# The end of the context attentions of a four-layer gated model: slot 0's head sums, inverses and output product placed between slot 1's column scores

## The chip, the cores and the metric

One core of one Trainium2 chip runs the whole program as one kernel. The metric is the device time of one execution in microseconds (us). TensorE is called PE below, VectorE DVE, ScalarE ACT.

## The reference, cut to what matters

Four gated blocks change `x` of 4 batches x 512 tokens x 128 features. Each block is a cross-attention on a context of 77 rows of 64 features, then a second function (a quantised MLP in the first block, others later). Blocks 0, 1 and 3 attend with 16 heads; block 1's context attention (`a2`) is the second half of a larger function and has 32 features a head, blocks 0 and 3 have 8.

```python
    x = x + jnp.tanh(g_xattn[0]) * _L0_xattn_ref(_layernorm(x, axis=-1), ctx_512, ctx_512, ...)
    x = x + jnp.tanh(g_ffn[0]) * _L0_ffn_ref(_layernorm(x, axis=-1), ...)
...
        scores = jnp.einsum('bhqd,bhkd->bhqk', qh, kh) * scale
        attn = jax.nn.softmax(scores, axis=-1)
        out = jnp.einsum('bhqk,bhkd->bhqd', attn, vh)
        concat = out.transpose(0, 2, 1, 3).reshape(B, LQ, D_MODEL)
        return concat @ Wo + bo
...
        h = layernorm(x, gamma, beta)
        h = qlinear(h, w1, b1)
        h = jax.nn.gelu(h, approximate=False)
        out = qlinear(h, w2, b2)
```

`qlinear` scales each token by the maximum of its absolute values, rounds, multiplies by rounded weights and scales back.

## The kernel before

The batches go through in two turns of a loop (`Fori`), two batches a turn; the two are slot 0 and slot 1 (`u`). Activations lie with features on the partitions and 512 tokens beside each other. Each engine has its own written-out program; an engine waits for another by a counter of finished steps (`TENSOR`, `SCALAR`, `VECTOR`), and the order on each engine is the order of its code. No planner or scheduler changes it.

A turn has three context attentions made by the function `cross(tag, dh)`, of which each of PE, ACT and DVE has one: `l0x` (`dh` 8), `a2` (`dh` 32) and `l3x` (`dh` 8). With two turns that makes six. In each, for a slot:

- `rowscores` (PE, L655 for `dh` 8, L659 for `dh` 32) computes scores with queries on the partitions, `maxima` (DVE, L1966) takes the row maxima, `turned` (PE, L668) and `shifted` (ACT, L1601) bring them to the other layout.
- `colscores4` (PE, L682) computes scores with keys on the partitions, 4 groups `k` of 4 heads, each 2 tiles of 2 PSUM banks, less the maxima; `exp` (ACT, L1610) takes a tile's exponentials.
- `values` (PE, L721) multiplies them with the values. For `dh` 8 the columns of ones beside the values give the sums; for `dh` 32 `sums` (PE, L707) gives them apart. ACT copies the results out (L1617; L1622 and L1621).
- The end, `dh` 8: `heads` (PE, L735) turns the sums to 64 numbers a token row, in two halves; `head_inverse` (DVE, L1994 and L1995) inverts them; `inverses` (PE, L745) turns them back; `divided` (DVE, L2001, in `l0x` also L2004) multiplies; `linear` (PE, L1030) is the output product with `Wo`; `residual` (DVE, L1929, in `l0x` also L1927) adds it to `xs`. In `l3x` the new `xs` is copied to `xall` (L2541) and the turn ends.
- The end, `dh` 32: `inverse` (DVE, L1979) inverts the sums; `spread` (PE, L793, four groups a slot) spreads them over the partitions; DVE multiplies (L2029); `reduce4` (PE, L1048) is the output product, joined over 4 chunks.

PSUM has 8 banks. `values` uses banks 0 and 1; the score tiles go round three pairs, banks 2 and 3, 4 and 5, 6 and 7, in the order of `cplace` and `cbank`, and `free(x)` makes PE wait until the tile three places earlier has been read. Slot 0's column scores alternate with slot 1's row scores. Slot 1's column scores then stand alone, with the end of slot 0 and of slot 1 behind them or between the last value products.

Behind `l0x` comes the quantised MLP, on DVE for the most part: the residuals of both slots are turned to token rows (PE, L1131), `token_norm` takes statistics (L2216, L2219) and applies them (L2224), then scale and quantise (L2298 to L2239), `turned back` (L2303) and the hidden values (L2307).

## Time and profile before

| what | value |
|---|---|
| time of 3 runs | 1881.96, 1880.04 and 1859.07 us, median 1880.04 |
| profiled execution | 1865.42 us, span of the core 1863.7 us |
| mean granted PE clock | 0.874 of full |
| busy: PE, DVE, ACT, POOL | 1597.1, 886.3, 728.7, 147.9 us |
| context attentions' ends, first turn (from slot 1's `turned` on) | `l0x` from 67.7 us, `a2` from 434.9, `l3x` from 822.5 |
| the same, second turn | `l0x` from 890.9 us, `a2` from 1250.7, `l3x` from 1638.4 |

The profile is of one execution, with the times of its own. A row of the timeline has its start, its length, the engine, the line of the kernel and, in brackets, how long the engine was idle before it and whose step ended that. PE's clock has two levels here: a PEclk of 0.50 is 1.2 GHz, of 1.00 is 2.4 GHz, and a number between them is a mean over a stretch that had both.

### The profile page before, as it was taken

The page shows a single profiled execution, that of the slowest core. Times are in us where ns is not written, and L with a number is a line of the kernel's source. Part 1 is how long each engine was busy: PE and PEld are TensorE (multiplying, and loading weights), DVE is VectorE, ACT ScalarE, POOL GpSimd, SP SyncE. Part 2 cuts the span into 40 slices and gives each one's busy share as a digit, 9 for nine tenths or more (in the row PEclk, how much of TensorE's full clock was granted, in tenths as well). Part 3 has the DMA queues.
Part 4 walks back from the last instruction along what each step waited for, and adds up shares of the span by engine and source line. Part 5 has one row for each costly group of instructions (what it writes and reads, how often), then busy time and mean ns, then how long its engine had stood idle before and what let it go on. Part 6 is the DMA issues. An engine that isn't in the chain of part 4 may idle for free.

```text
span 1863.7 us, 22238 instructions
## 1 busy us (share of the span) xinstructions
PE 1597.1 (86%) x8922; PEld 739.3 (40%) x8924; DVE 886.3 (48%) x1710; ACT 728.7 (39%) x1279; POOL 147.9 (8%) x207
## 2 busy tenths in 40 slices
PE   5948999879899989987659999898899989888387
PEld 2322323332344435733324322342444437543284
DVE  4283686253456343234555784342664442437312
ACT  2334555323545224242344554433454134243033
POOL 0000111100012000000000112000011000002321
PEclk8568899989999688987778999899998789889688
DMA  4000000000000100000000000000000100020241
GB/s 184 1 0 1 1 1 1 1 0 1 0 1 1 46 1 0 1 1 2 1 1 1 1 1 1 1 1 0 1 1 1 46 0 1 1 74 5 67 138 60
DMA packets 18106, 30.15 MB, mean 16 GB/s; under 512 B 4640, under 2 KB 12640, under 8 KB 17104
## 3 DMA queue, kind: packets, MB, share of 16 engines
q1 hardware_dynamic: 16752, 26.10, 4.3%
q0 software_dynamic: 1248, 2.59, 0.4%
q8 instruction: 73, 1.20, 0.3%
q14 instruction: 33, 0.27, 0.0%
HBM read 23.49 MB, written 5.19 MB: 15 GB/s over the span
## 4 chain that ended last, share of the span: by engine, by line
PE 77%; DVE 12%; ACT 7%; issue 2%; DMA 1%; POOL 1%; SPq 0%; POOLq 0%; DVEq 0%; ACTq 0%
PE ps L817 7%; PE ps L910 4%; PE ps L682 4%; PE ps L852 3%; PE ps L627 3%; PE ps L1356 3%; PE ps L1368 3%; PE ps L1040 3%; PE ps L721 3%; PE ps L961 3%; PE ps L941 2%; PE ps L865 2%; PE ps L1048 2%; PE ps L659 2%; PE ps L842 2%
## 5 line engine op out<-in xcount | busy, mean ns | idle before, releaser
L2039 DVE TENSOR_REDUCE peak<-ps 128x1 f32<-128x512 f32 x256 | 164.1, 686 | 93.6 <-PE ps L817 92.0
L1656 ACT ACTIVATE big<-ps 128x512 f32<-128x512 f32 x256 | 140.9, 595 | 125.1 <-PE ps L844 123.6
L842 PE MATMUL ps<-qT,pp 32*128 32x512 f32 x512 | 162.2, 659 | 0.0
L817 PE MATMUL ps<-pp,qT 32*128 32x512 f32 x512 | 150.7, 673 | 1.4 <-ACT pp L1762 1.4
L1679 ACT ACTIVATE big<-ps 128x512 f32<-128x512 f32 (+3 forms) x256 | 101.2, 437 | 116.8 <-PE ps L941 115.8
L2084 DVE TENSOR_REDUCE crest<-ps 128x2 f32<-128x512 f32 (+3 forms) x128 | 104.9, 825 | 61.6 <-PE ps L916 61.5
L941 PE MATMUL ps<-qT,pp 32*128 32x384 f32 (+3 forms) x512 | 130.7, 521 | 2.3 <-ACT big L1679 1.4
L1610 ACT ACTIVATE big<-ps 77x1024 f32<-77x1024 f32 x96 | 93.4, 1017 | 89.1 <-PE ps L682 88.6
L1966 DVE TENSOR_REDUCE small<-ps 128x8 f32<-128x616 f32 x96 | 74.3, 798 | 91.3 <-PE ps L655 53.5
L910 PE MATMUL ps<-pp,qT 32*128 32x384 f32 (+3 forms) x512 | 105.4, 480 | 5.3 <-DVE crest L2084 2.7
L1590 ACT ACTIVATE sq<-ps 128x512 f32<-128x512 f32 x48 | 28.7, 597 | 180.4 <-PE ps L627 180.4
L682 PE MATMUL ps<-qT,kt 32*77 32x512 f32 x384 | 84.2, 744 | 10.9 <-ACT spare L1601 9.6
L556 POOL TENSOR_SCALAR_AFFINE_SELECT big<-big 128x512 f32<-128x512 f32 x64 | 40.6, 634 | 586.9 <-PE ps L852 586.9
L574 POOL TENSOR_SCALAR_AFFINE_SELECT big<-big 128x512 f32<-128x512 f32 x64 | 41.2, 643 | 528.6 <-ACT big L1679 528.6
L817 PEld LDWEIGHTS ps<-pp,qT 32*128 32x128 f32 x512 | 47.6, 193 | 72.0 <-DVE peak L2039 41.7
L1040 PE MATMUL ps<-xn,w_l 128*128 128x512 f32 x96 | 55.4, 743 | 18.4 <-DVE xn L1923 18.4
L2054 DVE RECIPROCAL rs<-sq 128x128 f32<-128x128 f32 (+2 forms) x48 | 57.9, 1209 | 22.2 <-ACT sq L1666 22.2
L852 PE MATMUL ps<-big,cst 128*32 128x512 f32 x512 | 68.2, 605 | 0.0
L1918 DVE TENSOR_TENSOR xn<-ps,rs 128x512 f32<-128x512 f32 x36 | 24.9, 692 | 89.0 <-ACT rs L1596 89.0
L1817 ACT ACTIVATE big<-ps,w_l 128x512 f32<-128x512 f32 x64 | 44.0, 687 | 59.1 <-PE ps L1356 57.5
L941 PEld LDWEIGHTS ps<-qT,pp 32*128 32x128 f32 x512 | 54.5, 198 | 21.4 <-ACT big L1679 14.3
L1368 PEld LDWEIGHTS ps<-pt,big 128*128 128x128 f32 x512 | 59.4, 192 | 6.7 <-issue 6.7
(480 smaller groups left out, 2777.7 us busy)
## 6 DMA issues: line engine op xcount, KB each, us to landing
big<-in_w SPq DMA_DIRECT2D x23, 256.0 KB, 3.1
pt<-in_l2w SPq DMA_DIRECT2D x2, 2048.0 KB, 7.7
w_l<-in_l SPq DMA_DIRECT2D x1, 3086.0 KB, 17.2
pp<-in_w SPq DMA_DIRECT2D x1, 2048.0 KB, 9.8
big<-by_expert SPq DMA_DIRECT2D x23, 66.0 KB, 1.9
by_expert<-cst SPq DMA_DIRECT2D x1, 1472.0 KB, 16.0
cst<-in_const SPq DMA_DIRECT2D x1, 1299.0 KB, 5.7
w_l<-in_l SPq DMA_DIRECT2D x1, 1218.0 KB, 7.8
```

Source lines behind the costliest of these rows:

```text
L682: mm = pe.matmul(PSB[cbank(x) + b][0:KC, :], keys, query, start=not less, stop=less, tile_position=(32 * c, 0))
L817: pe.matmul(rbank(x), qT[at, u, k, 128 * i:128 * i + 128], keyT(u, k)[at, :], start=True, stop=True, tile_position=(32 * c, 0)).then_inc(* ...
L842: pe.matmul(tbank(y), keyT(u, k)[at, 128 * j:128 * j + 128], qT[at, u, k, :], start=True, stop=False, tile_position=(32 * c, 0))
L852: mm = pe.matmul(PSB[1][32 * c:32 * c + 32, :], K["ones"][:, 0:32], prob(n)[:, c, :], start=n % 4 == 0, stop=n % 4 == 3, tile_position=(0, ...
L910: pe.matmul(PSB[pbank(x) + c % 2][:, 0:hi], qT[at, u, k, 128 * i:128 * i + 128], keyT(u, k)[at, 0:hi], start=True, stop=False, tile_positi ...
L941: pe.matmul(tbank(y)[:, lo:512], keyT(u, k)[at, 128 * j:128 * j + 128], qT[at, u, k, lo:512], start=True, stop=True, tile_position=(32 * c ...
L1040: pe.matmul(scb(c), w[:, 128 * c:128 * c + 128], src(u), start=True, stop=True)\
L1368: mm = pe.matmul(lin(u)[:, 128 * i:128 * i + 128], hid[u][:, c, 128 * i:128 * i + 128], W2[:, 128 * c:128 * c + 128], start=c == 0, stop=c ...
L1656: A(prob(m)[:, TURN_OF[g], :], tbank(tplace(m, g)), ACT.Exp).then_inc(*SCALAR.did("a1", "exp", m, g))
L1679: A(prob(m)[:, TURN_OF[g], lo:512], tbank(tplace(m, g))[:, lo:512], ACT.Exp)\
L2039: v.tensor_reduce(peak[:, p // 4 % 2, i, c:c + 1], rbank(ring(p, c)), AX.X, ALU.max)\
L2084: v.tensor_reduce(crest[:, u, i, 2 * h:2 * h + 2, k], ps[:, b:b + 2, 0:hi], AX.X, ALU.max)\
```

## The change

Four things are done, in all six context attentions.

1. Slot 1's column scores go round two pairs of banks (6 and 7, 2 and 3) in place of three. The pair 4 and 5 is given to slot 0's end.
2. For `dh` 8, PE's program from slot 1's column scores on is written out: slot 0's two `heads`, its `inverses` and its output product (`outward`) stand between the groups of column scores and value products. The residual moves into DVE's `cross` too.
3. For `dh` 32, slot 0's `spread` stands behind slot 1's third and fourth group of column scores, and DVE multiplies slot 0 before it inverts slot 1's sums. Slot 0's joined output product (`outward4`) stands before slot 1's `spread`.
4. In `l0x`, slot 0's turn to token rows, statistics and norm move into `cross`, between slot 1's steps, and the stage behind is written out slot by slot. Banks for these change.

No DMA is added, removed or moved, and neither SP's nor POOL's program changes; the same instructions compute the same values.

PE in `l0x` (`l3x` has the same without L1131), from slot 1's second group of value products to its output product, that of both slots being one row before. Names: `qT` queries, `kt` keys, `spare` the shift, `big` exponentials, `vx` values, `xn` and `sq` what ACT kept, `rs` inverses, `cst` constants, `w_l` weights. Before:

```order
L721 MATMUL ps<-big,vx 32x512 x4
L682 MATMUL ps<-qT,kt 77x512 x4
L682 MATMUL ps<-spare,minus 77x512 x4
L721 MATMUL ps<-big,vx 32x512 x4
L735 MATMUL ps<-cst,xn 128x4x2 x4
L735 MATMUL ps<-cst,sq 128x4x2 x4
L721 MATMUL ps<-big,vx 32x512 x4
L735 MATMUL ps<-cst,xn 128x4x2 x4
L745 MATMUL ps<-cst,rs 128x128 x4
L735 MATMUL ps<-cst,sq 128x4x2 x4
L745 MATMUL ps<-cst,rs 128x128 x4
L1030 MATMUL ps<-xn,w_l 128x512 x2
```

After, from the same value products on:

```order
L742 MATMUL ps<-big,vx 32x512 x4
L766 MATMUL ps<-cst,rs 128x128 x4
L703 MATMUL ps<-qT,kt 77x512 x4
L703 MATMUL ps<-spare,minus 77x512 x4
L742 MATMUL ps<-big,vx 32x512 x4
L654 MATMUL ps<-xn,w_l 128x512
L742 MATMUL ps<-big,vx 32x512 x4
L756 MATMUL ps<-cst,xn 128x4x2 x4
L1178 MATMUL ps<-cst,xs 128x128 x4
L756 MATMUL ps<-cst,sq 128x4x2 x4
L766 MATMUL ps<-cst,rs 128x128 x4
L654 MATMUL ps<-xn,w_l 128x512
```

The head sums (L735, now L756) of slot 0, its inverses (L745, now L766) and its output product (L1030, now L654) have moved up between column scores (L682, now L703) and value products (L721, now L742). The two head sums of slot 0 stand above these rows, behind the first group of column scores and behind the first value products.

DVE in `l0x`, from slot 0's division on (`part` the joined values, `small` the inverses and statistics of a token row, `gate` the gates, `xs` the residual stream). Before:

```order
L2001 TENSOR_TENSOR xn<-part,ps 128x512
L2004 TENSOR_SCALAR xn<-xn,w_l 128x512
L1994 RECIPROCAL small<-ps 128x64
L1995 COPY rs<-small 128x512
L1989 SCALAR_TENSOR_TENSOR part<-sq,cst,part 128x512
L2001 TENSOR_TENSOR xn<-part,ps 128x512
L2004 TENSOR_SCALAR xn<-xn,w_l 128x512
L1927 TENSOR_SCALAR xn<-ps,w_l 128x512
L1929 SCALAR_TENSOR_TENSOR xs<-xn,gate,xs 128x512
L1927 TENSOR_SCALAR xn<-ps,w_l 128x512
L1929 SCALAR_TENSOR_TENSOR xs<-xn,gate,xs 128x512
L2216 BN_STATS small<-ps 128x6 x4
```

After:

```order
L2046 TENSOR_TENSOR xn<-part,ps 128x512
L2049 TENSOR_SCALAR xn<-xn,w_l 128x512
L1972 TENSOR_SCALAR xn<-ps,w_l 128x512
L1974 SCALAR_TENSOR_TENSOR xs<-xn,gate,xs 128x512
L2030 TENSOR_SCALAR part<-xn,cst 128x512
L2269 BN_STATS small<-ps 128x6 x4
L2272 BN_AGGR small<-small 128x2 x4
L2039 RECIPROCAL small<-ps 128x64
L2040 COPY rs<-small 128x512
L2034 SCALAR_TENSOR_TENSOR part<-sq,cst,part 128x512
L2278 TENSOR_SCALAR xn<-ps,small 128x128 x4
L2046 TENSOR_TENSOR xn<-part,ps 128x512
```

Slot 0's residual (L1927 and L1929, now L1972 and L1974), its statistics (L2216, now L2269) and its applied norm (now L2278) have moved ahead of slot 1's division (L2001, now L2046).

PE in `a2`, from slot 1's last group of column scores. Before:

```order
L682 MATMUL ps<-qT,kt 77x512 x4
L682 MATMUL ps<-spare,minus 77x512 x4
L707 MATMUL ps<-big,cst 32x512 x4
L721 MATMUL ps<-big,vx 32x512 x4
L707 MATMUL ps<-big,cst 32x512 x4
L721 MATMUL ps<-big,vx 32x512 x4
L793 MATMUL ps<-rs,cst 32x512 x32
L1048 MATMUL ps<-qT,w_l 128x512 x8
L627 MATMUL ps<-x,cst 128x512 x2
```

After:

```order
L703 MATMUL ps<-qT,kt 77x512 x4
L703 MATMUL ps<-spare,minus 77x512 x4
L821 MATMUL ps<-rs,cst 32x512 x8
L728 MATMUL ps<-big,cst 32x512 x4
L742 MATMUL ps<-big,vx 32x512 x4
L728 MATMUL ps<-big,cst 32x512 x4
L742 MATMUL ps<-big,vx 32x512 x4
L829 MATMUL ps<-qT,w_l 128x512 x4
L821 MATMUL ps<-rs,cst 32x512 x16
L829 MATMUL ps<-qT,w_l 128x512 x4
L644 MATMUL ps<-x,cst 128x512 x2
```

Half of the spreading (L793, now L821) and of the joined product (L1048, now L829) stands before slot 1's spreading; the other eight matmuls of slot 0's spreading stand two rows above the first shown.

The diff, cut to its core:

```diff
-                return a if u == 0 else 26 + a
+                return a if u == 0 else 26 + 3 * (a // 2) + a % 2
...
-                return "T", 1, z - 26
+                return "T", 1, 2 * ((z - 26) // 3) + (z - 26) % 3
...
+        def spread_bank(u, k):
+
+            return PSB[4 + k % 2] if u == 0 else PSB[2 + (4 + k) % 6]
+
+        def joined_bank(u):
+            return PSB[4] if u == 0 else PSB[1]
+
+        def ybank(u):
+
+            return PSB[4] if u == 0 else PSB[1]
+
+        def xtbank(u):
+            return PSB[5] if u == 0 else PSB[7]
+
+        def q1bank(u):
+            return PSB[4] if u == 0 else PSB[7]
 
...
-            def cross(tag, dh):
-
+            def cross(tag, dh, wo=None, tokens_first=None):
+
+
+                def outward(u):
+                    pe.wait_ge(*VECTOR[tag, "o", u])
+                    pe.matmul(ybank(u), wo, xn[:, u, :], start=True, stop=True).then_inc(*TENSOR.did(tag + " y", u))
...
                 def free_late(x):
-                    pe.wait_ge(*SCALAR[tag, "exp", 1, x - 29])
+                    pe.wait_ge(*(SCALAR[tag, "exp", 1, 6] if x == 35 else SCALAR[tag, "shift", 1]))
...
                 turned(1)
+                if dh == 8:
+                    colscores4(1, 0)
+                    heads(0, 0)
+                    colscores4(1, 1)
+                    values(1, 0)
+                    heads(0, 1)
+                    colscores4(1, 2)
+                    values(1, 1)
+                    inverses(0)
+                    colscores4(1, 3)
+                    values(1, 2)
+                    outward(0)
+                    values(1, 3)
+                    heads(1, 0)
+                    if tokens_first:
+                        tokens_first(0)
+                    heads(1, 1)
+                    inverses(1)
+                    outward(1)
+                    if tokens_first:
+                        tokens_first(1)
+                    return
+
+                def spread(u, k):
+                    pe.wait_ge(*VECTOR[tag, "inv", u])
+                    if u == 0 and k < 2:
+                        pe.wait_ge(*SCALAR[tag, "shift", 1])
+                    elif u == 0:
+                        pe.wait_ge(*VECTOR[tag, "O", 0, k - 2])
+                    for c in range(4):
+                        row = 32 * c + 8 * k
+                        mm = pe.matmul(spread_bank(u, k)[32 * c:32 * c + 32, :],
+                                       K["ident"][:, row:row + 1].to_broadcast([128, 32]), rs[:, u, :], start=True,
+                                       stop=True, tile_position=(0, 32 * c))
+                    mm.then_inc(*TENSOR.did(tag, "spread", u, k))
+
+                def outward4(u):
+                    for c in range(4):
+                        pe.wait_ge(*VECTOR[tag, "O", u, c if u else 3])
+                        mm = pe.matmul(joined_bank(u), wo[:, 128 * c:128 * c + 128], qT[:, u, c, :], start=c == 0, stop=c == 3)
+                    mm.then_inc(*TENSOR.did(tag + " li1", u))
+
                 for k in range(4):
                     colscores4(1, k)
+                    if k >= 2:
+                        spread(0, 2 * k - 4)
+                        spread(0, 2 * k - 3)
                     if k:
                         sums(1, k - 1)
                         values(1, k - 1)
-                if dh == 8:
-                    heads(0, 0)
-                    heads(0, 1)
                 sums(1, 3)
                 values(1, 3)
-                if dh == 8:
-                    heads(1, 0)
-                    inverses(0)
-                    heads(1, 1)
-                    inverses(1)
-                    return
-                for u in U:
-                    pe.wait_ge(*VECTOR[tag, "inv", u])
-                    for k in range(4):
-                        at = 4 * u + k
-                        if at >= 6:
-                            pe.wait_ge(*VECTOR[tag, "O", 0, at - 6])
-                        for c in range(4):
-                            row = 32 * c + 8 * k
-                            mm = pe.matmul(PSB[2 + at % 6][32 * c:32 * c + 32, :],
-                                           K["ident"][:, row:row + 1].to_broadcast([128, 32]), rs[:, u, :], start=True,
-                                           stop=True, tile_position=(0, 32 * c))
-                        mm.then_inc(*TENSOR.did(tag, "spread", u, k))
+                outward4(0)
+                for k in range(4):
+                    spread(1, k)
+                outward4(1)
...
+                def tokens_first(u):
                     pe.wait_ge(*VECTOR["l0x res", u])
                     for i in range(4):
-                        mm = pe.transpose(aux(u)[:, 128 * i:128 * i + 128], xs[:, u, 128 * i:128 * i + 128], ident)
+                        mm = pe.transpose(xtbank(u)[:, 128 * i:128 * i + 128], xs[:, u, 128 * i:128 * i + 128], ident)
                     mm.then_inc(*TENSOR.did("l0f xt", u))
+
+                cross("l0x", 8, W["l0"]["Wo"], tokens_first)
...
-                token_rstd("l0f a")
+                token_rstd("l0f a", 0)
                 act.wait_ge(*VECTOR["l0f rounded", 50, 0])
                 A(tq(0), xn[:, 0, :], ACT.Identity, bias=K["unmagic"]).then_inc(*SCALAR.did("l0f q1", 0))
+                token_rstd("l0f a", 1)
...
-            def cross(tag, dh, bv=None):
...
                 if dh == 8:
-                    for u in U:
-                        joined(u, 0)
-                        if u:
-                            divided(0)
-                        else:
-                            joined(0, 1)
-                            head_inverse(0)
+                    joined(0, 0)
+                    joined(0, 1)
+                    head_inverse(0)
+                    divided(0)
+                    residual_of(0)
+                    joined(1, 0)
+                    if tokens:
+                        stats, applied, scaled = tokens
+                        stats(0)
                     head_inverse(1)
                     joined(1, 1)
+                    if tokens:
+                        applied(0)
                     divided(1)
+                    residual_of(1)
+                    if tokens:
+                        scaled(0)
                     return
                 for u in U:
                     inverse(u)
-                for u in U:
+                    if u:
+                        residual_of(0)
                     for k in range(4):
                         v.wait_ge(*TENSOR[tag, "spread", u, k])
                         v.wait_ge(*SCALAR[tag, "o", u, k])
-                        v.tensor_tensor(qT[:, u, k, :], qT[:, u, k, :], PSB[2 + (4 * u + k) % 6], ALU.mult)\
+                        v.tensor_tensor(qT[:, u, k, :], qT[:, u, k, :], spread_bank(u, k), ALU.mult)\
                             .then_inc(*VECTOR.did(tag, "O", u, k))
+                residual_of(1)
...
-                for u in U:
+
+                def residual_of(u):
                     v.wait_ge(*TENSOR["l0x y", u])
-                    residual("l0x res", u, lin(u), 0, W["l0"]["bo"])
-
-                for u in U:
+                    residual("l0x res", u, ybank(u), 0, W["l0"]["bo"])
+
...
-                for u in U:
+
+                def turned_back(u):
                     v.wait_ge(*TENSOR["l0f q1T", u])
-                    v.tensor_copy(xq(u), aux(u).bitcast(BF16)[:, 0:512]).then_inc(*VECTOR.did("l0f xq", u))
-                for u in U:
+                    v.tensor_copy(xq(u), q1bank(u).bitcast(BF16)[:, 0:512]).then_inc(*VECTOR.did("l0f xq", u))
+
+                def hidden_of(u):
                     for i in range(4):
                         v.wait_ge(*TENSOR["l0f h", u, i])
                         v.scalar_tensor_tensor(hid[u][:, i, :], scb(i), sm(u, 50 + i, 1), W["l0"]["b1r"], ALU.mult,
                                                ALU.add).then_inc(*VECTOR.did("l0f h", u, i))
+
+                cross("l0x", 8, residual_of, W["l0"]["bv"], (stats, applied, scaled))
+                stats(1)
+                turned_back(0)
+                applied(1)
+                hidden_of(0)
+                scaled(1)
+                turned_back(1)
+                hidden_of(1)
...
-                cross("a2", 32)
-                for u in U:
+
+                def joined(u):
                     v.wait_ge(*TENSOR["a2 li1", u])
-                    v.scalar_tensor_tensor(x2[:, u, :], lin(u), w["a2_li1_b"], x1[:, u, :], ALU.add, ALU.add)\
+                    v.scalar_tensor_tensor(x2[:, u, :], joined_bank(u), W["l1"]["a2_li1_b"], x1[:, u, :], ALU.add, ALU.add)\
                         .then_inc(*VECTOR.did("a2 x2", u))
+
+                cross("a2", 32, joined)
```

## Rows read from the trace of the kernel before

**Rows 1.** The page: busy time of each engine, and the chain that ended last.

```profile
PE 1597.1 (86%) x8922; PEld 739.3 (40%) x8924; DVE 886.3 (48%) x1710; ACT 728.7 (39%) x1279; POOL 147.9 (8%) x207
...
PE 77%; DVE 12%; ACT 7%; issue 2%; DMA 1%; POOL 1%; SPq 0%; POOLq 0%; DVEq 0%; ACTq 0%
```

**Rows 2.** Timeline of `l3x`, first turn, from slot 1's shift: start us, us, engine, line, operation.

```profile
823.00 0.60 ACT L1601 ACTIVATE spare<-ps 128x512 bf16<-128x512 bf16 x1 [1.73 <-PE ps L668]
...
825.09 1.93 ACT L1610 ACTIVATE big<-ps 77x1024 f32<-77x1024 f32 x2 [1.48 <-PE ps L682]
...
826.16 0.66 PE L682 MATMUL ps<-qT,kt 32*77 32x512 f32 x2 [0.25 <-ACT big L1610]
...
832.08 1.93 ACT L1610 ACTIVATE big<-ps 77x1024 f32<-77x1024 f32 x2 [0.42 <-PE ps L682]
...
833.02 1.06 PE L735 MATMUL ps<-cst,xn 128*128 128x8 f32 x8
...
834.90 1.07 PE L721 MATMUL ps<-big,vx 77*32 77x512 f32 x8
...
835.90 1.88 PE L735 MATMUL ps<-cst,xn 128*128 128x8 f32 x8
...
837.63 2.06 PE L745 MATMUL ps<-cst,rs 128*128 128x128 f32 x8
...
842.30 2.07 PE L745 MATMUL ps<-cst,rs 128*128 128x128 f32 x8 [1.11 <-DVE rs L1995]
...
844.17 2.83 PE L1030 MATMUL ps<-xn,w_l 128*128 128x512 f32 x4
...
848.03 0.43 DVE L2541 COPY xall<-xs 128x512 f32 x1
```

**Rows 3.** Busy time by stretch; the PEclk column is the granted clock's share of full.

```profile
40.00:84.00 44.00, 42.05 (x188) 12.87 (x192) 7.98 (x12) 16.50 (x19) 0.00 (x0) 0.50 0.00 1
823.00:836.00 13.00, 12.00 (x97) 4.73 (x97) 1.71 (x4) 9.17 (x11) 0.00 (x0) 0.99 0.00 1
836.00:845.00 9.00, 7.89 (x33) 7.30 (x34) 3.35 (x7) 0.60 (x1) 0.00 (x0) 0.50 0.00 0
...
446.60:450.00 3.40, 3.40 (x24) 0.77 (x20) 0.00 (x0) 0.89 (x1) 0.00 (x0) 0.52 0.00 0
```

**Rows 4.** Timeline of `a2`, first turn, from slot 1's shift.

```profile
435.38 0.60 ACT L1601 ACTIVATE spare<-ps 128x512 bf16<-128x512 bf16 x1 [1.49 <-PE ps L668]
...
445.67 1.06 PE L721 MATMUL ps<-big,vx 77*32 77x512 f32 x8 [1.50 <-ACT qT L1622]
...
454.24 3.62 PE L793 MATMUL ps<-rs,cst 128*32 128x512 f32 x32
...
455.12 3.35 DVE L1979 RECIPROCAL rs<-sq 128x512 f32<-128x512 f32 x1 [11.87 <-ACT sq L1621]
...
458.52 3.64 PE L793 MATMUL ps<-rs,cst 128*32 128x512 f32 x32 [0.67 <-DVE rs L1979]
...
462.09 7.13 PE L1048 MATMUL ps<-qT,w_l 128*128 128x512 f32 x16
```

**Rows 5.** Timeline of `l0x` and the stage behind it, second turn.

```profile
891.35 0.60 ACT L1601 ACTIVATE spare<-ps 128x512 bf16<-128x512 bf16 x1 [1.73 <-PE ps L668]
...
916.83 0.75 DVE L1929 SCALAR_TENSOR_TENSOR xs<-xn,gate,xs 128x512 f32<-128x512 f32 x1
...
918.40 0.89 DVE L2216 BATCH_NORM_STATS2 small<-ps 128x6 f32<-128x128 f32 x4 [0.82 <-PE ps L1131]
...
920.81 2.61 DVE L2224 TENSOR_SCALAR xn<-ps,small 128x128 f32<-128x128 f32 x8
...
923.46 0.69 DVE L2298 TENSOR_TENSOR xn<-xn,w_l 128x512 f32<-128x512 f32 x1
...
927.29 0.69 DVE L2298 TENSOR_TENSOR xn<-xn,w_l 128x512 f32<-128x512 f32 x1
...
932.68 5.36 DVE L2307 SCALAR_TENSOR_TENSOR big<-ps,small,w_l 128x512 f32<-128x512 f32 x8
```

72 lines of the change are left out of this document (33 added, 39 removed).

## Prediction

> **What bounds the kernel now.** I read the page first. PE is busy 1597.1 us and has 77% of the chain that ended last; DVE has 12% and ACT 7% [rows 1]. So a gain has to shorten PE's program or a wait of PE's, and the six context attentions have both. The timeline of `l3x` shows it. From slot 1's shift on, ACT's four pairs of exponentials start at 825.09 and last at 832.08, three steps of 2.33 us, each pair 1.93 us long: ACT and PE hand over without much of a gap. Then PE does alone what is left: head sums at 833.02, the last value product at 834.90, head sums at 835.90, inverses at 837.63, 842.30 and the output products at 844.17, until DVE's last copy ends at 848.46 (848.03 and 0.43) [rows 2]. Counted from the end of the shift (823.60), the exponentials end at 10.4 and the attention at 24.9 us: 14.5 us lie behind the last exponential. The view by stretch shows another thing in this end: the granted clock is 0.99 from 823 to 836 and 0.50 from 836 to 845, so full rate (2.4 GHz) while scores are computed, half (1.2 GHz) in the head sums and inverses [rows 3]. In `a2` the end is one of full products: from slot 0's spreading at 454.24, over DVE's inverse of slot 1 (455.12, 3.35 us), slot 1's spreading at 458.52 (3.64 us) and the joined product of both slots at 462.09 (7.13 us), it ends at 469.2 [rows 4].
>
> No DMA is issued in these stretches and neither SP's nor POOL's program moves, so only PE, ACT and DVE count. I take `l3x` and `a2` of one turn for both, since their programs are the same, and correct for the clock.
>
> **`a2`, two times.** Removed from behind slot 1's sums is half of the joined product, 7.13 / 2 = 3.57 us: slot 0's half now runs while DVE takes slot 1's inverse of 3.35 us, in which PE before did slot 0's spreading (3.62 us) [rows 4]. Slot 1's spreading and its half product stay behind the inverse, 3.6 + 3.6 us, and DVE's multiplications of slot 1 (8 of them took 4.81 us before, so 0.6 each) run beside the spreading; the residual of slot 0 (0.75 us by the same operation as in [rows 5]) delays the first by less than the spreading lasts. Slot 0's spreading is moved into the column scores, where PE waited 1.50 us for ACT's copy [rows 4] before the second value product, so that half of its 3.6 us of work, at least, finds an idle PE. Against the gain stands the third pair of banks. The second group of column scores now waits for both exponentials of the first group. In `l3x` PE waited for the first alone and went on at 826.16, 0.10 us after its end (825.09 and half of 1.93) [rows 2]; the second ends 0.97 later. In `a2` ACT has two copies of 0.6 us (the row at 435.38 shows the size of one) between these pairs, which cover all but about 0.3 us of it. With this and what of the moved spreading is not covered I take 0.5 us off: 3.57 - 0.5 = 3.1 us each, 6.2 in all. The ends are 1.9 each, when the half clock at 446.60 (0.52 [rows 3]) comes back in the moved spreading, and 3.7, when the wait that stood before it is filled and the clock stays full.
>
> **`l3x`, two times.** Removed from the place behind the last exponential is slot 0's share: its inverse (1.7 us at half clock, as the half head sum from 835.90 to 837.63 [rows 2]), its output product (half of the 2.83 us at 844.17 [rows 2], and more where PE waits), and of its head sums what ran past 834.0. Added is that the column scores now go in lockstep with the exponentials. I set the steps out from the shift's end, by the rows' durations. The pair of exponentials starts at 1.5 and ends at 3.4. PE's products then need about 1.05 us (0.10 us of release, 0.66 us [rows 2] and the subtraction behind it), ACT's copy of slot 0 (0.60) falls in this gap, and pair 2 starts at 4.5 and ends at 6.4. PE has in the meantime to do a value product of 1.0 (834.90 to 835.90) and a half head sum of 0.94 (833.02 to 834.90 are two) [rows 2], and is free at 6.3; column scores and two releases take 1.4 (from the shift's end, 823.60, to the first exponential at 825.09 it is 1.49), so pair 3 starts at 7.7 and ends at 9.6. Value product, inverse (1.2 at full rate, which no row shows, between 0.94 and 1.7) and column scores give pair 4 a start at 11.2 and an end at 13.2, against 10.4 before: 2.8 us later. Behind it come, each with its release, a value product (1.1), two half head sums at full rate (0.95 and 1.15), DVE's inverse and copy (1.1), PE's inverse at half clock (2.2), a division (0.8), the output product at half clock (2.05), residual and copy (1.2, of which 0.43 is a row [rows 2]): 10.5 us where there were 14.5. The sum is 13.2 + 10.5 = 23.7 against 24.9, a gain of 1.2 us. If the clock falls as early as before (at 836, which is 12.3 after the shift [rows 2, 3]), both head sums cost 1.7 in place of 0.94, the last value product doubles and the gain is a loss of 1.3 us; if it stays full to the end, inverse and output product are 1.6 us shorter and the gain is 2.7. The clock fell 2.9 us after slot 0's head sums began (833.02 to 836 [rows 2, 3]), and these no longer stand together, so I expect the fall later than before; between 1.2 and -1.3 I take 0.5 each, 1.0 in all.
>
> **`l0x`, two times.** The same to the end of slot 1's residual, and with three things in DVE's and PE's way: slot 0's residual (1.5 us by two steps of 0.75), its statistics of 1.2 (918.40 to 920.81 are two), its applied norm of 1.3 (2.61 for two) [rows 5]. Slot 1's inverse on PE waits behind the first two for DVE's inverse of slot 1, about 0.9 us later; the norm stands before slot 1's division, beside PE's inverse of 2.1 us, and sticks out by 0.7. So slot 1's residual ends 25.6 us after the shift, as before (917.58 less 891.95). Behind it, DVE had 20.4 us to the end of the hidden values (917.58 to 938.04) [rows 5]. Now it has slot 0's scaling 3.8 (923.46 to 927.29), slot 1's statistics 1.3, norm 1.3 and scaling 4.2 (with one more step of 0.43), hidden values of 5.4, two copies of 0.4 and about 2 us of waits for PE's turning and ACT's rounding, which slot 0 covered for slot 1 before: 18.7 us. The gain is 1.7 us, with the ends 3.0 (clock full throughout) and -1.5 (clock falls as early as before). I take 1.2. In the first turn `l0x` runs at half clock from 40 to 84 us (0.50, PE busy 42.05 of 44.00 [rows 3]); PE is the bound all along there, so that only DVE's share comes through and slot 1's residual comes later: 0.3. In all 1.5.
>
> **The sum** is 6.2 + 1.0 + 1.5 = 8.7 us. ACT gets no new work; its one added order, slot 0's rounding before slot 1's root, waits for nothing that is late.
>
> **The page that speaks against it.** The rows show PE at 0.52 right after it waited 1.50 us in `a2`, while at 1.00 or 0.99 elsewhere in the scores [rows 3, 4]. The Trainium skill, "TensorE: Matmul & The Clock Gate", section "A second HAM failure mode: psum-queue depth-cycling", says that matmul groups that cycle through PSUM banks with small idle times between them make the clock go back and forth between its two levels. By that rule a ring of two pairs in place of three, with PE waiting in each step, would lose the clock in the column scores; that is the second case below. The trace bears it out once in each `a2`.
>
> **The cases.**
>
> - *Forecast, 0.50.* A gain of 8.7 us. With all terms at their lower ends it is -0.3 (2 x 1.9 - 2 x 1.3 - 1.5), at their upper ones 16.
> - *The clock falls within slot 1's column scores, 0.18: slower.* Place: from the second group on, since PE then waits in each step for exponentials. Price, from the ladder above: with value products of 1.9 and column scores of 2.4 in place of 1.0 and 1.3 the last exponential of `l3x` ends at 16.7 in place of 13.2, and the end at half clock (by the same steps at half clock, 14.4) gives 31.1 against 24.9, 6.2 us lost; `l0x` of the second turn loses 5.4, that of the first nothing more, `a2` gains 1.9. Together 2 x 6.2 + 5.4 - 2 x 1.9 = 14 us slower. An `l3x` end that runs so costs 6.7 us against the forecast, so the sign turns from two such ends on. For it: 0.52 in [rows 3]. Against it: PE's waits here are short, at most 1 us, and the moved work fills them.
> - *The third pair is worth as much as the moved work, 0.17: no change.* The clock falls at the same place as before in each `dh` 8 attention (-1.3, -1.3, -1.5, 0) and `a2` gains 2.4 each: 0.7 us faster. For it: the exponentials' spacing of 2.33 us [rows 2] becomes 3.2.
> - *The clock holds to the end, 0.15.* All terms at their upper ends: 2 x 2.7 + 3.0 + 0.3 + 2 x 3.7 = 16 us faster; should the first turn's `l0x` also escape the half clock, up to some 15 us more (at most half of the 42.05 us [rows 3], an estimate), 31 in all.
>
> That the instructions don't move is no case: order and waits are fixed by the written program.
>
> **How the numbers follow.** The profiled execution took 1865.42 us (its span and 1.7 around it), so by its own time the changed kernel takes 1856.7. The three runs shown have the median 1880.04 and lie at 1859 and near 1881, so the profile is one of the faster executions; the first turn's `l0x` at half clock, or not, could alone make such a gap. I set the sum against the middle of all four executions, (1865.4 + 1880.0) / 2 = 1872.7: 1872.7 - 8.7 = 1864. The cases then lie at 1864, 1887, 1872 and 1857 (to 1842). The forecast's own range, its ends with 4 us for the middle that I chose, is 1852 to 1877; to hold 8 in 10 it takes in both outer cases, 1842 to 1887. Two per cent, about what a measurement of this kernel can tell from no change, is 37.6 us from 1880, so faster means under 1842.4: only the last case with its escape, and a fast draw of the forecast, 0.08. Slower means over 1917.6, which the second case does not reach without a slow draw on top, 0.02. The rest is 0.90.
>
> **What the profile of the changed kernel would show.** In `l3x`, pairs of exponentials 3 to 3.5 us apart in place of 2.33, and no PE work of slot 0 behind the last of them. In `a2`, slot 0's joined product beside DVE's inverse of slot 1, a wait of about 1 us, then slot 1's spreading and 3.6 us of product. In `l0x`, DVE with hidden values of slot 0 before slot 1's scaling, and the second hidden values ending some 44 us after the shift. The clock of the stretches in [rows 3] decides among the cases: 0.50 before the last exponential is the second, at the same place as before the third, 1.00 to the output product the fourth. The prediction is wrong if the exponentials are much further apart at full clock, if PE's heads and inverses cost more between column scores than alone, or if the clock of work outside the attentions changes too.

## The result and the profile after

The changed kernel takes 1881.01 us in the median of 20 runs (1850.04 to 1907.58), the kernel before beside it 1859.21 us (20 runs, 1843.13 to 1881.96); the ratio is 1.0087, with an interval from 1.0053 to 1.0120. That is less than 2%, but it is a loss, where a gain of 8.7 us was forecast. Ratios here leave out runs more than 1.5% above the fastest of their kernel (seven of twelve in e7 below), medians hold all runs, so where a kernel's times spread widely the two can differ.

The runs of one kernel don't scatter about one value. Their time goes with the mean granted clock: the changed kernel gave 1850 us at a clock of 0.875, 1866 at 0.864, 1875 at 0.861, 1888 at 0.852, and 1906 to 1908 at 0.840 four times. At one clock the changed kernel is the faster: at 0.875 it took 1850 and 1854 us, the kernel before 1865. So the question is why its clock is lower.

The profiled execution of the changed kernel took 1866.13 us (span 1864.4), at a clock of 0.864; that of before 1865.42 (1863.7) at 0.874. The page of the changed kernel, busy time, granted clock in 40 slices and the chain that ended last; the shares are those of [rows 1] to 2%:

```profile
PE 1606.3 (86%) x8924; PEld 733.9 (39%) x8924; DVE 887.9 (48%) x1710; ACT 729.8 (39%) x1279; POOL 147.9 (8%) x207
...
PEclk9558999989899689996568999899898789889688
...
PE 79%; DVE 11%; ACT 6%; issue 2%; DMA 1%; POOL 1%; SPq 0%; POOLq 0%; DVEq 0%; ACTq 0%
```

**What was worked out is there.** The timeline of `l3x`, first turn, from slot 1's shift, against [rows 2]:

```profile
817.03 0.60 ACT L1646 ACTIVATE spare<-ps 128x512 bf16<-128x512 bf16 x1 [1.73 <-PE ps L689]
...
819.12 1.93 ACT L1655 ACTIVATE big<-ps 77x1024 f32<-77x1024 f32 x2 [1.48 <-PE ps L703]
...
822.25 1.93 ACT L1655 ACTIVATE big<-ps 77x1024 f32<-77x1024 f32 x2 [0.72 <-PE ps L703]
...
826.55 1.16 PE L766 MATMUL ps<-cst,rs 128*128 128x128 f32 x8
...
829.03 1.93 ACT L1655 ACTIVATE big<-ps 77x1024 f32<-77x1024 f32 x2 [1.45 <-PE ps L703]
...
835.07 1.16 PE L766 MATMUL ps<-cst,rs 128*128 128x128 f32 x8 [1.11 <-DVE rs L2040]
...
837.01 2.07 PE L654 MATMUL ps<-xn,w_l 128*128 128x512 f32 x2 [0.78 <-DVE xn L2046]
...
839.91 0.43 DVE L2612 COPY xall<-xs 128x512 f32 x1
```

The exponentials now start 3.1 to 3.4 us apart in place of 2.33, slot 0's inverse (L766 at 826.55) stands between column scores at full rate, and from the end of the shift (817.63) to the last copy (840.34) it is 22.7 us where it was 24.9: 2.2 us gained, where 0.5 was forecast.

The timeline of `a2`, first turn, against [rows 4]:

```profile
432.60 0.60 ACT L1646 ACTIVATE spare<-ps 128x512 bf16<-128x512 bf16 x1 [1.48 <-PE ps L689]
...
451.19 3.70 PE L829 MATMUL ps<-qT,w_l 128*128 128x512 f32 x8
451.96 3.35 DVE L2024 RECIPROCAL rs<-sq 128x512 f32<-128x512 f32 x1 [3.44 <-ACT sq L1666]
...
455.37 3.64 PE L821 MATMUL ps<-rs,cst 128*32 128x512 f32 x32 [0.47 <-DVE rs L2024]
458.94 3.70 PE L829 MATMUL ps<-qT,w_l 128*128 128x512 f32 x8
```

Slot 0's joined product (451.19) lies beside DVE's inverse of slot 1 (451.96), PE waits 0.47 us, spreads, and ends at 462.6: 29.4 us from the shift's end where it was 33.2, 3.8 us gained for 3.1 forecast.

**Where it is lost.** Busy time of the changed kernel by stretch. The column after the five engines is the granted clock. The first line is `l0x` of the first turn (first row scores at 33.2) from where the clock falls to where it is back; the second and third are `l3x` of the first turn, from the first row scores at 790.4 to the fall and from there until it is back; the fourth is `l0x` of the second turn (first row scores at 855.9), fall to return.

```profile
37.80:89.00 51.20, 47.85 (x218) 18.58 (x220) 12.71 (x21) 16.21 (x19) 0.00 (x0) 0.50 0.00 1
790.40:795.60 5.20, 4.82 (x33) 2.17 (x32) 5.08 (x8) 0.00 (x0) 0.00 (x0) 0.99 0.00 0
795.60:802.40 6.80, 4.15 (x22) 1.82 (x20) 1.81 (x5) 1.62 (x2) 0.00 (x0) 0.50 0.01 2
...
860.40:911.60 51.20, 47.86 (x218) 18.51 (x220) 12.83 (x22) 16.12 (x18) 0.00 (x0) 0.50 0.00 1
```

That last attention of the kernel before, `l0x` in the second turn, first row scores at 864.7:

```profile
864.70:870.00 5.30, 4.92 (x33) 2.19 (x32) 5.20 (x8) 0.00 (x0) 0.00 (x0) 1.00 0.00 0
870.00:876.80 6.80, 4.11 (x22) 1.87 (x22) 1.80 (x5) 1.64 (x3) 0.00 (x0) 0.50 0.00 0
876.80:904.10 27.30, 24.72 (x196) 9.26 (x196) 8.60 (x14) 16.44 (x19) 0.00 (x0) 1.00 0.01 1
```

In every one of these attentions the clock falls to 1.2 GHz about when slot 0's row scores end. Mostly it is back at 2.4 GHz after 7 us; in `l0x` of the first turn in both kernels, and of the second turn in the changed one alone, it stays at half for 51 us (48 in the kernel before), through both slots' scores. I call this a stay. The changed kernel began its second turn 8.0 us ahead (first product of the norm of `l0x` at 847.1 against 855.1) and was 6.4 us behind at the next norm (961.5 against 955.1): 14.4 us lost in a stretch of which the row scores, where the clock falls, are not changed at all. (The end of the attention and the token stage behind it, in the same stretch, are changed.)

### The profile page after: what moved, and what is told of

Read it like the earlier page. It is cut to its first block, busy times and chain, and to the rows that moved or that the text cites. A ratio compares the mean times of both kernels' runs of the same rounds, so it can differ in the third digit from the quotient of the medians.

```text
span 1864.4 us, 22242 instructions
## 1 busy us (share of the span) xinstructions
PE 1606.3 (86%) x8924; PEld 733.9 (39%) x8924; DVE 887.9 (48%) x1710; ACT 729.8 (39%) x1279; POOL 147.9 (8%) x207
## 4 chain that ended last, share of the span: by engine, by line
PE 79%; DVE 11%; ACT 6%; issue 2%; DMA 1%; POOL 1%; SPq 0%; POOLq 0%; DVEq 0%; ACTq 0%
PE ps L866 7%; PE ps L959 5%; PE ps L703 4%; PE ps L901 3%; PE ps L644 3%; PE ps L1402 3%; PE ps L1414 3%; PE ps L742 3%; PE ps L1089 3%; PE ps L1010 2%; PE ps L990 2%; PE ps L914 2%; PE ps L1317 2%; PE ps L891 2%; PE ps L680 2%
## 5 line engine op out<-in xcount | busy, mean ns | idle before, releaser
L959 PE MATMUL ps<-pp,qT 32*128 32x384 f32 (+3 forms) x512 | 110.4, 501 | 4.5 <-DVE crest L2138 2.3
L703 PE MATMUL ps<-qT,kt 32*77 32x512 f32 x384 | 87.3, 795 | 12.0 <-ACT spare L1646 9.6
L1963 DVE TENSOR_TENSOR xn<-ps,rs 128x512 f32<-128x512 f32 x36 | 24.9, 692 | 89.1 <-ACT rs L1641 89.1
L1089 PE MATMUL ps<-xn,w_l 128*128 128x512 f32 x96 | 49.3, 673 | 18.0 <-DVE xn L1968 18.0
```

What stands on the lines that cost most here:

```text
L703: mm = pe.matmul(PSB[cbank(x) + b][0:KC, :], keys, query, start=not less, stop=less, tile_position=(32 * c, 0))
L959: pe.matmul(PSB[pbank(x) + c % 2][:, 0:hi], qT[at, u, k, 128 * i:128 * i + 128], keyT(u, k)[at, 0:hi], start=True, stop=False, tile_positi ...
L1089: pe.matmul(scb(c), w[:, 128 * c:128 * c + 128], src(u), start=True, stop=True)\
```

## The experiments

Three theories. **A**: the change is a gain at equal clock; it loses because more of the four `dh`-8 attentions stay at half clock, and what decides is the moment at which the clock falls against the row scores, set by what ran before. **B**: the ring of two pairs, or the changed end, costs by itself. **D** (formed on the way): the new order of the token stage behind `l0x` costs half clock there. The C in the expectations of e1 and e2, that the clock of later stages reacts to when they start, became the second half of A.

**e1, the `a2` part alone.** The kernel before, and of the diff the lines for `dh` 32:

```diff
-                return a if u == 0 else 26 + a
+                return a if u == 0 else 26 + (a if dh == 8 else 3 * (a // 2) + a % 2)
...
-                cross("a2", 32)
-                reduce4("a2 li1", w["a2_li1"], lambda u: qT[:, u, :, :],
+                cross("a2", 32, w["a2_li1"])
```

> The kernel before with the change made in the dh-32 context attention (a2) alone; the two dh-8 attentions of each turn stay as before. Theory A (the moved work is a gain at equal clock, and the loss of the whole change sits in dh-8 attentions that stay at half clock more often): the a2 stage is some 4 to 5 us shorter in each of the two turns, the dh-8 attentions are as before, so about 9 us off the time, 1850 us where the before is 1859, with no a2 stretch below a granted clock of 0.95. Rival B (the two-pair score ring costs wherever it is used): within 2 us of the before, or slower. Rival C (the clock of later stages reacts to when they start): anything from 1850 to 1880, with the extra time in a dh-8 attention at granted clock 0.50, not in a2.

**e2, the `dh`-8 part alone.** The changed kernel with `cross` for `dh` 32 and its places as before:

> The changed kernel with its dh-32 attention (a2) put back to three pairs of score banks and the old order; the dh-8 attentions stay changed. Theory A: this part carries the loss. At equal clock it would be some 6 us faster than the before, but about 1.5 more of the four dh-8 attentions stay at half clock, at about 14 us each, so 1870 to 1890 us where the before is 1859. Rival B (two-pair ring costs everywhere): half of the changed kernel's difference, 1865 to 1872. Rival C (only the timing of the start decides which attentions stay slow): between 1845 and 1885, not told apart from the before on the mean.

**e3 and e4, fillers** in the changed kernel and in the kernel before:

```diff
+                def kept_busy(n):
+                    if dh == 8:
+                        for _ in range(n):
+                            pe.matmul(PSB[0], identb[:], w1q[:], start=True, stop=True)
...
                 for a in range(8):
                     rowscores(0, a)
+                    if a >= 2:
+                        kept_busy(5 if a == 7 else 2)
                 turned(0)
+                kept_busy(3)
```

> The changed kernel with filler products on TensorE in the dh-8 attentions alone: two bf16 products of 512 columns after each of slot 0's row scores from the third, five after the last and three after the turned queries, all into a bank that nobody reads. They fill the idle time ahead of the first column scores. Theory A (the loss is attentions that fall to, or stay at, half clock because TensorE idles between row and column scores): all four dh-8 attentions but perhaps the first run at full clock, the repeats agree within 0.5%, and the time is 1845 to 1855 us. Rival B (the change costs by itself, by the ring or by queueing): 1875 us or more, as the fillers can only add. If the fillers are late behind the row scores, each attention is up to 2 us longer instead.

> The kernel before with the same filler products in the same places. Theory A: its one stay at half clock of four goes too, 1845 to 1855 us, and the changed kernel with fillers is then 5 to 16 us faster than this one, which is what the change is worth at equal clock. Rival B: the changed kernel with fillers is not faster than this one, and the gap of the pair is that of the pair without fillers, some 15 us the other way.

Measured on one chip, kernel before 1859.4: e1 1859.6 us (12 runs, 1837 to 1887; ratio 0.9959, 0.9911 to 1.0008), e2 1872.6 (12 runs, 1851 to 1884; 1.0059, 1.0013 to 1.0105), e3 1843.0 (8 runs, 1838 to 1846; 0.9933, 0.9888 to 0.9978), e4 1843.6 (12 runs, 1836 to 1851; 0.9913, 0.9882 to 0.9944). The fillers take 38 us off the changed kernel, by adding work, and most of its spread: B has it falling by nothing, so B is out as the main cause. e2's 1872.6 us lies inside A's 1870 to 1890 and a hair above B's 1865 to 1872, and so hardly tells them apart. Both with fillers are equal, which A didn't expect: at equal treatment the change is worth about nothing, not 5 to 16 us; its clock is the lower one still (0.887 to 0.890 against 0.889 to 0.901). e1 missed A's 1850 us and has the median of the kernel before. It is also broader (clock 0.856 to 0.889), although its `dh`-8 attentions are untouched: its two slowest runs, at 1887 us, lie above all 31 runs of before beside it (1870 at most) and just above the slowest of before in any comparison (1884). Its profile has no stay, so that these runs have more of them is inferred from their clock alone.

**e5 and e6, the rows 0.75 us later.** By then six profiles gave 16 attentions without fillers, and the falls that came before 5 us were those that stayed. So the moment was moved, in the kernel before and in the changed one:

```diff
+                if dh == 8:
+                    pe.wait_ge(*VECTOR[tag, "kv", 0])
+                    pe.wait_ge(*VECTOR[tag, "q", 0])
+                    for _ in range(3):
+                        pe.matmul(PSB[0], identb[:], w1q[:], start=True, stop=True)
                 for a in range(8):
                     rowscores(0, a)
```

> The kernel before, and in each of its four dh-8 attentions TensorE does three filler products (0.25 us each, 0.75 us together) ahead of the first row scores; nothing else differs. In the six profiles so far the granted clock falls to half once, 4.4 to 5.8 us after the first row scores begin, in each of the 16 attentions without fillers: where it falls at 4.4 to 4.8 it stays at half for 48 to 51 us, at 5.2 or later it is back within 17. Theory A (the moment of that fall against the rows decides, and it is fixed by what ran before): with the rows 0.75 us later it falls at 4.5 where it fell at 5.2 or 5.3, so three or four attentions of four stay at half clock: 1890 to 1905 us, clock near 0.85, from a change worth 3 us by itself. Rival B (something in the changed end of the attention makes it stay): this kernel has the old end and is 1860 to 1863 us.

> The changed kernel with the same three filler products ahead of the first row scores of its dh-8 attentions. Theory A: all four attentions stay at half clock in most runs, 1900 to 1910 us, what the slowest runs of the changed kernel show, with little spread. Rival B: the changed kernel's median and 3 us, 1876 to 1884, with its spread.

**e7, a pause elsewhere.** Twenty of these products ahead of the joined product of `a2`, after a wait for slot 1's last multiplication, in the kernel before:

> The kernel before with twenty filler products (5 us, at full clock) ahead of the joining product of its dh-32 attention, once in each turn; all else is as before. Theory A with shifts that carry over (what runs before moves the later falls of the clock): the extra is not 10 us but 10 us and a changed number of attentions at half clock, so a clock below or above 0.875 and a time outside 1866 to 1872. Theory A with falls that are tied anew to each attention by the work just ahead of it: 1869 us, with the stays of the dh-8 attentions as in the kernel before.

**e8, fillers and the `a2` part alone**, the edits of e1 and e4 together:

> The kernel before with the change in the dh-32 attention alone, and the filler products of the earlier pair in its dh-8 attentions. If the changed end of the dh-8 attentions is worth something at equal clock (some 1 to 2 us each), this is 2 to 8 us slower than the changed kernel with fillers (1843). If instead the new order of the token stage behind l0x costs, as the stage from l0x to l1's first norm says (101.6 us against 99.1 in the first turn, 95.3 against 98.4 in the second), they come out equal, 1838 to 1846.

Measured, kernel before 1856.8: e5 1900.1 us (6 runs, 1890 to 1924; ratio 1.0249, 1.0180 to 1.0317), e6 1888.7 (7 runs, 1888 to 1905; 1.0193, 1.0139 to 1.0246), e7 1891.9 (12 runs, 1852 to 1910; 1.0055, 0.9997 to 1.0112), e8 1837.4 (12 runs, 1829 to 1849; 0.9934, 0.9897 to 0.9971). Twelve products of 0.25 us, 3 us of work, cost the kernel before 43 us. Its profile by stretch, `l3x` in the first turn (793.95, a stay now) and `l0x` in the second (878.95, none):

```profile
793.95:798.65 4.70, 4.32 (x31) 2.06 (x32) 4.02 (x7) 0.00 (x0) 0.00 (x0) 1.00 0.00 0
798.65:846.45 47.80, 44.47 (x196) 13.08 (x196) 10.37 (x17) 17.83 (x20) 0.00 (x0) 0.50 0.00 1
...
878.95:884.00 5.05, 4.67 (x33) 2.19 (x32) 4.43 (x7) 0.00 (x0) 0.00 (x0) 1.00 0.00 0
884.00:890.80 6.80, 4.40 (x24) 1.82 (x20) 2.04 (x5) 1.39 (x2) 0.00 (x0) 0.50 0.01 2
```

Its fall came 4.7 us after the first row in the one and 5.0 in the other. The second turn's `l3x` fell at 4.6 and stayed too. Its first `l0x` is an exception: the fall came late, at 7.1 us, and 41 us at half clock followed all the same, with PE busy in nearly all of them.

```profile
33.75:40.90 7.15, 4.93 (x34) 2.20 (x33) 6.39 (x11) 0.00 (x0) 0.00 (x0) 1.00 0.00 0
40.90:81.90 41.00, 39.06 (x172) 12.10 (x172) 7.98 (x12) 15.88 (x18) 0.00 (x0) 0.50 0.00 1
```

e6 has a stay in all four attentions; two of them, with falls at 4.2 and 4.9 us:

```profile
795.70:799.90 4.20, 3.82 (x29) 1.87 (x28) 3.52 (x6) 0.00 (x0) 0.00 (x0) 1.00 0.00 0
799.90:851.10 51.20, 47.86 (x216) 18.41 (x212) 12.54 (x21) 16.10 (x18) 0.00 (x0) 0.50 0.00 1
880.30:885.20 4.90, 4.45 (x31) 2.18 (x32) 4.21 (x7) 0.00 (x0) 0.00 (x0) 1.00 0.01 2
885.20:936.40 51.20, 47.78 (x216) 18.12 (x218) 12.36 (x21) 16.65 (x19) 0.00 (x0) 0.50 0.00 1
```

e6's median, 1889, is under the forecast of 1900 to 1910: most of its runs, at 0.854, have one stay less than the profiled one at 0.845 by the scale of the other kernels. e7 points the same way but doesn't show it: two pauses of 5 us in `a2` raised the median by 35 us, yet its ratio gives a loss of 0.55%, the 10 us of the pauses and no more. Its profile has two stays (falls at 4.2 and 4.5 us), that of the kernel before one. e8 was to be 2 to 8 us slower than e3 or equal to it, and came out 5.6 us faster, in another comparison.

**e9 to e12.** e9 is e3 with the token stage behind `l0x` in the old order (`tokens_first` out of `cross`, and statistics, norm, scaling, copies and hidden values for both slots one after the other). e10 is e8 and more fillers, `kept_busy(4)` ahead of `inverses(1)`, `kept_busy(3)` behind it, 20 behind `l3x y`. e11 repeats e8. e12 is e3 without the fillers between rows:

```diff
-                    if a >= 2:
-                        kept_busy(5 if a == 7 else 2)
+                    if a == 7:
+                        kept_busy(5)
```

> The changed kernel with the filler products of the first pair, and the token stage behind l0x (transposes, statistics, rounding) put back into the order of before: both slots through each step after the attention, in place of slot 0's steps beside slot 1's heads. In the profiles with fillers the stretch from l0x's norm to l1's first took 101.6 and 95.3 us with the changed kernel's dh-8 attentions and 99.1, 98.4, 97.9 and 97.8 with those of before, and the token stage stood at half clock for 41 us on end against 14 and 14 with full clock between. If the new token order causes that (theory D), this kernel has the broken stretch again and is 2 to 6 us faster than the changed kernel with fillers, about 1839. If the order is a gain, as it was meant, it is 1 to 3 us a turn slower, 1845 to 1849.

> The kernel before with the change in the dh-32 attention alone and the fillers between and after the row scores (1837 us when last run), and in addition four fillers ahead of slot 1's joining of the inverse, three ahead of the joining product and twenty behind l3x's joining product, where TensorE is idle for 1.1, 0.8 and 6.2 us. If the clock falls at the end of the attention because of these idle times, the half-clock stretches of 10 to 14 us that begin 39 to 50 us after the first row become shorter or vanish: 1825 to 1835. If not, the same as without them, 1837, or a few us slower where the fillers run at half clock and are late.

> The kernel before with the change in the dh-32 attention alone and fillers in the dh-8 attentions, unchanged from its first run, now beside the others on one chip: 1837 us, clock 0.897, 17 to 22 us under the median of the kernel before.

> The changed kernel with fillers only behind the last row scores of slot 0 (five) and behind the turned queries (three), none between the row scores. If the fall of the clock, 4.4 to 5.8 us after the first row, comes from the small idle times between the row scores, it still falls; what then matters is whether the stay comes from the idle time that follows. If that idle time makes the stay, the clock is back within 17 us in all four attentions, 1850 to 1856. If the moment of the fall alone decides, the stays are as in the changed kernel without fillers, 1870 to 1890.

Measured, kernel before 1863.3: e9 1837.6 us (6 runs, 1827 to 1841; ratio 0.9877, 0.9822 to 0.9931), e10 1846.2 (12 runs; 0.9929, 0.9895 to 0.9963), e11 1841.9 (12 runs, 1829 to 1849; 0.9910, 0.9875 to 0.9945), e12 1844.6 (12 runs, 1830 to 1847; 0.9952, 0.9913 to 0.9991). e10 is 4 us slower than e11 beside it: the idle time at the end of the attentions isn't worth filling so. e12 was expected at 1850 to 1856 or, if the moment of the fall alone decides, at 1870 to 1890; it is faster than both. So filling the idle time behind the last row scores is enough to take the stays away. Its `l0x` of the second turn, and the last two rows its `l3x` of the second turn:

```profile
839.80:844.90 5.10, 4.65 (x33) 2.20 (x32) 4.93 (x7) 0.00 (x0) 0.00 (x0) 1.00 0.01 2
844.90:848.30 3.40, 3.07 (x14) 1.31 (x12) 2.00 (x5) 0.22 (x1) 0.00 (x0) 0.50 0.00 0
848.30:868.80 20.50, 17.72 (x141) 7.43 (x141) 7.22 (x11) 10.68 (x13) 0.00 (x0) 1.00 0.00 1
...
1584.10:1589.00 4.90, 4.52 (x33) 2.19 (x32) 4.74 (x7) 0.00 (x0) 0.00 (x0) 1.00 0.00 0
1589.00:1592.40 3.40, 3.06 (x13) 1.30 (x11) 2.12 (x5) 0.00 (x0) 0.00 (x0) 0.50 0.00 0
```

The clock falls at 5.1 us in the one and at 4.9 in the other, where without fillers a stay followed at up to 4.9, and is back after 3.4 us in both. In the changed kernel without fillers PE stood idle here in two places; its timeline of PE in `l0x`, second turn, where the clock fell at 860.4:

```profile
857.68 4.22 PE L676 MATMUL ps<-kt,qT 32*128 32x308 f32 x20 [0.45 <-DVE small L2011]
863.31 0.61 PE L689 MATMUL ps<-identb,spare 128*128 128x128 bf16 x4 [1.41 <-DVE spare L2019]
864.69 2.08 PE L703 MATMUL ps<-qT,kt 32*77 32x512 f32 x6 [0.78 <-ACT spare L1646]
```

**e13 to e16**, the old token order with e12's fillers, e12's fillers in the kernel before, the changed kernel once more, and the changed kernel with nothing but the old token order:

> The changed kernel with the token stage behind l0x in the old order, and fillers only behind slot 0's last row scores (five) and behind the turned queries (three), in the dh-8 attentions. Theory A and D together: no stays at half clock, no 41 us of half clock in the token stage, no delay from fillers between rows (2.3 us an attention): 1826 to 1838 us, below every other kernel here. If D is wrong: 1844, as the same fillers gave with the new token order.

> The kernel before with the same eight fillers in each dh-8 attention, five behind the last row scores and three behind the turned queries. Theory A: its stays go too, 1838 to 1845 us. The gap from this to the changed kernel with these fillers and the old token order is what the change's other parts are worth with no stays: 6 to 14 us by the stage times (a2 3.5 a turn, its two clock dips 3 to 4 a turn less 2.3 behind it, the dh-8 ends 1 to 2 each).

> The changed kernel as it is, once more. 1870 to 1888 us in the median, clock near 0.86; in the profile at least two of the four dh-8 attentions are at half clock for about 50 us, in each of them the clock falls less than 5.0 us after the first row scores begin, in the others later.

> The changed kernel with only the token stage behind l0x put back into the old order, no fillers. Theory D: 3 to 6 us faster than the changed kernel beside it at the same number of stays, so 1866 to 1884, with the stays left in (clock about 0.865). If the token order were the main cause of the loss: the kernel before's median or less, under 1862.

Measured, kernel before 1858.0: e13 1836.1 us (12 runs, 1826 to 1843; ratio 0.9914, 0.9878 to 0.9950), e14 1836.2 (12 runs, 1831 to 1839; 0.9920, 0.9893 to 0.9947), e15 1876.0 (6 runs, 1845 to 1886; 1.0150, 1.0072 to 1.0229), e16 1865.9 (12 runs, 1840 to 1889; 1.0030, 0.9974 to 1.0086). The profile of e15 is not what was expected: it is its fastest run (1845 us) and has no stay at all. So the same program is free of them in one execution and has two in another, and its falls are late, as the theory wants; `l0x` of the first and of the second turn:

```profile
34.50:40.50 6.00, 4.88 (x33) 2.15 (x32) 5.87 (x9) 0.00 (x0) 0.00 (x0) 1.00 0.01 1
40.50:50.70 10.20, 8.16 (x40) 3.88 (x40) 2.66 (x5) 3.48 (x4) 0.00 (x0) 0.50 0.01 2
846.90:852.80 5.90, 4.92 (x33) 2.19 (x32) 5.75 (x9) 0.00 (x0) 0.00 (x0) 1.00 0.01 1
852.80:863.10 10.30, 8.13 (x38) 3.89 (x40) 2.79 (x6) 3.44 (x4) 0.00 (x0) 0.50 0.01 2
...
897.20:938.20 41.00, 16.78 (x96) 11.11 (x95) 32.05 (x79) 13.75 (x16) 0.00 (x0) 0.50 0.00 0
```

The last line is theory D's: the token stage behind `l0x`, 41 us at half clock on end, with PE busy in 16.78 of them. The profile of e13 has full clock for 3.5 us within it, and then half for 13.6:

```profile
846.10:849.50 3.40, 3.07 (x10) 1.20 (x12) 2.48 (x5) 0.00 (x0) 0.00 (x0) 0.50 0.00 0
849.50:887.10 37.60, 32.77 (x254) 14.48 (x251) 14.41 (x24) 18.80 (x22) 0.00 (x0) 1.00 0.00 1
907.50:911.00 3.50, 0.69 (x2) 0.10 (x1) 3.50 (x6) 2.32 (x2) 0.00 (x0) 0.99 0.00 0
911.00:924.60 13.60, 5.31 (x49) 5.05 (x50) 9.81 (x19) 8.91 (x11) 0.00 (x0) 0.50 0.00 0
```

Its fall at 846.1 came 4.7 us after the first row, where a stay would have followed; with the fillers it is back after 3.4 us.

The clock bears D out in every profile. All 12 turns of the six kernels with the new token order (the changed kernel, e2, e3, e6, e12, e15) have 41 us at half on end there. None of the 28 turns with the old order has more than 34 us on end, and 21 of them have 3.4 us of full clock in the middle and then 14 us at half. In time, e16 against e15, 10 us less in the median, goes D's way, but both are broad. Two more pairs differ in the token order alone, each across two comparisons: e3 and e9 (1843.0 and 1837.6) and e12 and e13 (1844.6 and 1836.1). So the new token order costs something like 5 to 10 us by these three pairs. In this comparison that is more than half of the loss: e15 lies 18 us above the kernel before, e16 8 us, and e16's interval holds 1, so that what is left of the loss without the token order isn't clear of noise here. e14 missed A's forecast: the gap between it and e13 was to be 6 to 14 us and is nothing.

**e17 and e18**, fillers of e12 with the `a2` part alone, and e13 again beside it:

> The kernel before with the change in the dh-32 attention alone, and five fillers behind the last row scores and three behind the turned queries of its dh-8 attentions. By the mean stage times of the profiles the a2 part is worth 2 us a turn from a2 to l3x (4.1 and 1.6 gained, most given back behind it), so 1832 beside 1836 for the kernel before with these fillers. If the part is worth the full 4 to 5 us a turn: 1826 to 1828. If its gain is all given back: 1836.

> The changed kernel with the old token order and the same eight fillers, unchanged, beside the kernel with the a2 part alone. If the dh-8 ends are worth what l3x shows with no stay (1.5 to 2.2 us in each turn, and nothing in l0x), this is 3 to 4 us faster than its neighbour. If the early end of slot 0 only moves the clock's later stretches, they are equal within 2 us: 1832 to 1837 both.

Measured, kernel before 1857.5: e17 1838.9 us (12 runs, 1836 to 1843; ratio 0.9958, 0.9926 to 0.9990), e18 1834.7 (12 runs, 1827 to 1842; 0.9939, 0.9906 to 0.9972). With no stays the `dh`-8 ends are worth about 4 us beside the `a2` part (e18 against e17). The `a2` part alone gains nothing that shows: 1838.9 here, where 1832 was expected, and 1836.2 for e14 in the comparison before. The two together are 1.5 us under e14.

**All attentions in one table.** From the granted clock in the nine profiles of kernels that have no filler behind a row score, 36 `dh`-8 attentions: how long after the first row scores the clock fell, and how long it then was at half.

| the fall after the first row scores | attentions | at half clock |
|---|---|---|
| 4.2 to 4.9 us | 14 | all 14 for 48 to 51 us |
| 5.0 to 6.0 us | 20 | 7 us (14) or 10 to 17 us (6) |
| 7.1 and 8.6 us | 2 | 41 us (e5's first) and 7 us |

In e12, e13, e14, e17 and e18, with fillers in the idle time alone, eleven falls came at 4.2 to 4.9 us, and none was followed by more than 7 us. Three came at 5.1 to 5.2, and six attentions had none before 36 us. In the six profiles with fillers between the row scores too (e3, e4 and e8 to e11) no attention of 24 had a fall before 31 us.

The table is of what goes together. e5 and e6 moved the fall from the late to the early side by products ahead of the rows, and stays came, in one profile each. That the moment itself makes the stay, and not something that sets both, is not shown. That filling the idle time behind the rows takes the stays away is shown, by eleven early falls of eleven.

## Why the prediction was wrong

**The step that failed** is the one that took the granted clock of the stages from one profile and priced the change in each stage by itself ("I take `l3x` and `a2` of one turn for both, since their programs are the same, and correct for the clock"). The clock in an attention doesn't belong to the attention. In 35 of 36 attentions it goes with whether its fall comes before or after about 5 us into the row scores, and this changes with what ran ahead: e5 put 0.75 us of products ahead of each and lost 43 us, and one and the same changed kernel has two stays in one execution and none in another (e15). The prediction's last sentence named the possibility ("if the clock of work outside the attentions changes too"), but no case carried it. That the measured 1881 us lies near its slow case (1887), and so inside its outer range, is luck, since the mechanism of that case is wrong: the clock doesn't fall within slot 1's column scores for the ring of two pairs. So the rule of the Trainium skill that was cited beside it ("TensorE: Matmul & The Clock Gate", section "A second HAM failure mode: psum-queue depth-cycling") isn't borne out in the column scores here: `a2` of the changed kernel, with the shallower ring, ran at full clock from its shift to its end and lost the dip to 0.52 of [rows 3]:

```profile
433.20:462.50 29.30, 27.59 (x193) 8.34 (x194) 12.78 (x11) 11.34 (x15) 0.00 (x0) 1.00 0.00 1
```

**The price of a stay.** From the first product of the norm of `l0x` to that of the next norm the changed kernel took 102.6 us without one (e15, both turns) and 114.5 and 114.3 with one: 12 us. From the norm of `l3x` in the first turn to PE's first product of the second turn it took 64.4 (first profile) and 65.2 (e15) without and 82.2 with one (e6): 17 us. The changed kernel has none in e15's profile at clock 0.880, two in its first at 0.864, and e6 has four at 0.845. On that scale (0.009 for each) its 20 runs, with a mean clock of 0.856, have 2.7 stays in the mean; the kernel before has one at 0.874, and its 31 runs beside e1, with a mean of 0.880, have 0.3. So 2.4 more at 12 us or more are at least 29 us, and the medians differ by 22. The scale is rough: it is drawn through a few profiles, and the four runs at 0.840 would have more than four stays by it, where there are four attentions to stay in. So it doesn't show that the 7 us between 29 and 22 are a hidden gain. That the stays are what costs most is shown by the kernels in which they are gone: e3 and e4, in one comparison, are equal. With the fillers behind the rows alone, the change without its token order is worth 0 to 1.5 us (e13 and e18 against e14; with fillers between the rows too, e9 against e4 in different comparisons, 6 us), and the whole change costs 8 us (e12 against e14, in different comparisons; 0.9952 and 0.9920 by the ratios). Why the changed kernel falls early more often than the kernel before was not found: no run separates the end of the attention, the token order and chance in that.

**`a2`, 3.1 us each.** The term was right where it was worked out, and given back behind it. Three stretches of the two profiles, `a2`, its norm and MLP, and `l1f`, the second function of block 1, up to the next norm; before:

```profile
381.80:469.10 87.30, 76.75 (x400) 30.32 (x399) 33.89 (x43) 25.41 (x34) 0.00 (x0) 0.90 0.00 1
469.10:494.10 25.00, 20.47 (x44) 8.10 (x42) 7.68 (x12) 12.37 (x17) 0.00 (x0) 0.93 0.00 0
494.10:677.80 183.70, 176.41 (x1163) 81.35 (x1163) 99.34 (x192) 68.36 (x161) 20.59 (x32) 0.87 0.03 12
```

and after:

```profile
381.90:462.50 80.60, 72.27 (x400) 28.53 (x399) 34.49 (x43) 25.54 (x34) 0.00 (x0) 0.95 0.00 1
462.50:485.80 23.30, 18.78 (x43) 7.51 (x41) 7.66 (x12) 12.38 (x17) 0.00 (x0) 1.00 0.00 0
485.80:671.80 186.00, 179.18 (x1163) 81.99 (x1163) 99.49 (x192) 68.49 (x161) 20.58 (x32) 0.85 0.03 12
```

6.7 us less, 1.7 less (the clock's dips are gone), and 2.3 more in a stage that isn't touched, at 0.85 for 0.87. It isn't chance: `l1f` took 186 to 187.5 us in 23 of the 24 turns of the twelve profiles up to e16 that have the new `a2`, and 181 to 183.7 in all twelve with the old one. Leaving out e7, the means are 85.5 and 81.4 us for `a2`, and 404.8 and 402.8 from `a2` to `l3x`: of 4 us and more, 2 a turn are left there. In the whole time not even these show (e17 against e14, above).

**`l3x`, 0.5 us each**, was mis-sized: 2.2 us by the timeline. The ladder of the forecast came out to 0.2 us as far as the last exponential (it starts 11.4 us behind the shift's end, for 11.2). The clock then stayed full through the head sums and slot 1's inverse (1.16 us in place of the 2.2 of the sum) and fell at 836.5, so that only the output product ran at half (2.07 us, for 2.05): between the forecast and the fourth case. The early fall of the clock, for which the ladder's 1.2 us were taken down to 0.5, didn't come. **`l0x`, 1.2 and 0.3 us,** failed: without a stay the stretch to the next norm takes 102.6 us, against 99.9 to 104.0 in the five such turns of kernels with the old end. Its second part, slot 0's token steps ahead of slot 1's, was priced as a gain and costs 5 to 10 us by the three pairs above. The token stage's 41 us at half clock, with PE busy in 16.78 of them (e15), are a term that the prediction didn't have.

**The middle.** Setting the sum against 1872.7 was off too: the kernel before has its median at 1857 to 1863 in all six comparisons; the 1880 of the three runs shown first was its slow end.

## What to carry to other kernels

Where the granted clock goes up and down within stages, ask of a profile first how many stages sit at half clock and how near each is to the other side, and repeat the run before trusting any single stage: here 0.75 us of products ahead of each of four stages cost 43 us, more than any reordering of work in the kernel gained. Where TensorE idles 2 to 3 us between two phases of a stage and the clock falls there, eight small products that nobody reads are a cheap trial; they took 22 us off the kernel before (e14, 1836.2), and the changed one with them and the old token order (e13 and e18, 1834.7 to 1836.1) is 40 us faster than it was. Judge a reordering beside its baseline with both made steady in this way: without its token order this one is then worth 0 to 1.5 us, 6 by one pair, with it between 0.6 us (e3 against e4) and a loss of 8 us (e12 against e14).

## What was not expected of the hardware

The clock's fall about 5 us into the row scores sorts the attentions into 7 to 17 us or some 50 us at half clock, with 0.1 us between the two sides (4.9 and 5.0 in the table) and one exception in 36 (7.1 us, then 41 us at half). In a stay PE is busy 47.86 of 51.20 us and the clock doesn't come back. In the first 6.8 us after the fall the two kinds look much alike, and the stay is the busier one:

```profile
860.40:867.20 6.80, 4.61 (x22) 2.27 (x24) 2.70 (x6) 0.65 (x2) 0.00 (x0) 0.50 0.00 0
```

PE is busy in 4.61 of 6.80 us here, where 44 us more at half clock follow, and in 4.15 of 6.80 us after the late fall of `l3x` (795.60 above), where the clock comes back. What sets the moment of the fall in the first `l0x`, where nothing of the kernel has yet differed (4.6 us in one execution of the changed kernel, 6.0 in another), stays open: no run here controls it. Why `l1f` runs at 0.85 behind the shorter `a2` wasn't tried either.
